# Image token products of a two-layer cross-attention on four column tiles, in two parts, with their weights loaded earlier

## The chip, the core and the metric

The kernel runs on one core of a Trainium2 chip. A core has five engines that work side by side and wait for one another by semaphores: TensorE (PE, with its weight loads listed as PEld), VectorE (DVE), ScalarE (ACT), GpSimd (POOL) and SyncE (SP, which here issues nearly all DMAs). The metric is the device time of one execution in microseconds, as a median of runs. TensorE's clock is granted at one of two levels, 2.4 GHz (1.00 in the rows) or 1.2 GHz (0.50).

## The reference

Two cross-attention layers over 8 batches of 256 tokens with 320 channels, 20 heads of 16; the context has 256 tokens with 512 channels. Layer 0 attends to the first 77 and to the other context tokens separately and adds the two. Layer 1 attends to the first 252 tokens, and to the last four (the image tokens) in a way of its own:

```python
k_ip = heads(ip_ehs @ W_k_ip)
v_ip = heads(ip_ehs @ W_v_ip)
attn_scores = jnp.einsum('bhsd,bhnd->bhsn', q, k_ip) * attn_scale
qsem = jnp.einsum('bhst,bte->bhse', probs_t, text_ehs)
qsem = _l2norm(qsem)
ip_n = _l2norm(ip_ehs)
sem = jnp.einsum('bhse,bne->bhsn', qsem, ip_n)
...
fused = attn_scores + SEM_SCALE * sem
probs_ip = jax.nn.softmax(fused, axis=-1)
...
ip_out = jnp.einsum('bhsn,bhnd->bhsd', probs_ip, v_ip)
```

The image tokens of all batches are 8 x 4 = 32 rows of 512 channels. Three small results are made of them once: their keys and values by two 512x320 weights, and their norms. The change is about these.

## The kernel before, in words

The work is cut into 16 units, eight batches of layer 0 and eight of layer 1. Each unit has ten slots j = 0 to 9; slot (u, j) handles the scores and weights of two heads of unit u, and beside them the maxima of the heads of unit u+1 and the projections of unit u+2. `plan(u, j)` (L80) writes out by hand what stands in a slot, and every engine walks through the same plan, each taking its own part of an item: PE multiplies, ACT takes exponentials (`P`) and copies results out of PSUM, DVE takes maxima and subtracts for the low parts, POOL does other differences, and SP stores queries and keys to DRAM and loads them back by heads. Nothing is reordered at run time. PE's results go to seven PSUM banks that are taken in turn; `take` waits until the earlier user of a bank has been read.

The image tokens are one item, `ip`, in slot (1, 3), behind everything else of that slot. Its function on PE is `image_tokens` (L612). For each of the two weights it makes three groups of output rows (128, 128, 64), each a sum of four matmuls with 128 rows of contraction and 32 moving columns (L620). Then come four matmuls that sum the squares `csq` over the partitions by a matrix of ones (L627), and four matmuls that give the values a second time with the tokens on the partitions (L632). All these are float32, and each such matmul appears in the trace as two instructions. ACT copies the results to `kip`, `vhi` and `vip`, DVE makes `vlo` and clips the norms (`nrm`), and POOL takes their power -0.5 (`invip`, L1329). Keys and norms are first used in layer 1.

The weights `wki1` and `wvi1` lie in the tile `Y` (128x3072), which layer 0 otherwise leaves free after the start. SP loads them (2 x 640 KB, L1357) at slot (0, 8), behind the rows of the shift (`QP<-mlo`, L746) and ahead of the key rows of unit 2 (`KP<-k0d`, L730), which the first maximum of slot (1, 0) needs (L458). Other names of the steps: L379 are the projections, L481 the scores, L513 and L517 the weighted values of a pair of slots, in which four heads stand on four column tiles of the array (`tile_position=(0, 32 * j)`), L536, L549, L553 and L469 transposes, L579 the output products of the unit before.

Of the kernel before, what the change touches and what calls it, by code (L numbers as in the profile page):

```python
# [9 lines left out]
ALU = mybir.AluOpType  # L10
# [7 lines left out]
NIP = 4  # L18
KC = 3
# [20 lines left out]
MAXF = (3, 3, 3, 3, 2, 2, 2, 2, 0, 0)  # L40
SHIFT = 7


# [36 lines left out]
def plan(u, j):  # L80
# [90 lines left out]
def build(nc, xT, cT, cipT, fs, Wq0, Wk0, Wv0, Wki0, Wvi0, Wo0, bo0,  # L171
          Wq1, Wk1, Wv1, Wki1, Wvi1, Wo1, bo1, ident_d, ind_d, hm_d, outT):
    with ExitStack() as ctx:
# [62 lines left out]
        kip = sb("kip", [128, KC, B * NIP])  # L236
        vhi, vlo = (cs[:, 96 * i:96 * i + 96].bitcast(F32R).rearrange("p (k n) -> p k n", n=B * NIP) for i in range(2))
        hmask = cs[:, 192:192 + KC * H].rearrange("p (k h) -> p k h", h=H)
        VB_all = sb("VB", [128, NIP * C])
        VB = VB_all[:, :].rearrange("p (n c) -> p n c", c=C)  # L240
        invip = sb("invip", [128, B * NIP])
        nrm = sb("nrm", [128, B * NIP])
        bdh, bdl = (VB_all[:, 240 * i:240 * i + 240].bitcast(F32R).rearrange("p (k h n) -> p k h n", k=KC, h=H) for i in range(2))
# [4 lines left out]
        rn = sb("rn", [128, 2, H])  # L248
        t1 = sb("t1", [128, 2, H, NIP])
        ex = sb("ex", [128, 2, H, NIP])  # L250
# [73 lines left out]
        def tensor_program(_):  # L324
# [5 lines left out]
            def freed(what):  # L330
                kind, a = what[0], what[1]
                if kind == "mx":
                    pe.wait_ge(dv_mx, a + 1)
                elif kind == "bg":
                    pe.wait_ge(ac_bg, job_no(a, what[2]))
                    if what[2] in LOWS[lay(a)]:
                        pe.wait_ge(dv_bg, low_no(a, what[2]))
                    if what[2] in ("G0", "G1"):
                        pe.wait_ge(dv_vg, 2 * (a - B) + 1 + (what[2] == "G1"))
                elif kind == "sc":  # L340
                    pe.wait_ge(ac_exp, 2 * a + what[2] + 1)
                elif kind == "gp":
                    pe.wait_ge(dv_y, 2 * (a - B * NP) + what[2] + 1)
                elif kind == "idle":
                    pass
                elif kind == "nt":
                    pe.wait_ge(dv_nb, a + 1)
                elif kind == "sr":
                    pe.wait_ge(ac_sr, a + 1)
                    pe.wait_ge(dv_sr, a + 1)  # L350
                elif kind == "ot":
                    pe.wait_ge(ac_ot, 2 * a + what[2] + 1)
                    pe.wait_ge(dv_ot, 2 * a + what[2] + 1)
                elif kind == "wt":
                    pe.wait_ge(ac_wt, closing_no(a))
                elif kind == "op":
                    pe.wait_ge(dv_op, 2 * a + what[2] + 1)
                elif kind == "mb":
                    pe.wait_ge(ac_mb, closing_no(a))
                elif kind == "ip":  # L360
                    pe.wait_ge(*((ac_ip, 1), (dv_ip, 1), (dv_ip, 2), (ac_ip, 3))[a])

# [248 lines left out]

            def image_tokens():  # L612
                for i, w in enumerate((wki1, wvi1)):
                    bank = take("ip", i)
                    pe.wait_ge(l_w["ip1"], 32)
                    pe.wait_ge(l_w["const"], 16 * 6)
                    for m in range(KC):
                        M = CHUNK[m]
                        for k in range(EC):
                            made = mm(bank[0:M, 32 * m:32 * m + 32], w[:, k, m * 128:m * 128 + M], cip[:, k, :],  # L620
                                      start=(k == 0), stop=(k == EC - 1))
                    made.then_inc(pe_ip, 1)
                    give(bank)
                bank = take("ip", 2)
                pe.wait_ge(dv_set, 3)
                for k in range(EC):
                    made = mm(bank[:, 0:32], ones[:, :], csq[:, k, :], start=(k == 0), stop=(k == EC - 1))  # L627
                made.then_inc(pe_ip, 1)
                give(bank)
                bank = take("ip", 3)  # L630
                for k in range(EC):
                    made = mm(bank[0:B * NIP, 0:C], cip[:, k, :], wvi1[:, k, :], start=(k == 0), stop=(k == EC - 1))  # L632
                made.then_inc(pe_ip, 1)
                give(bank)

# [10 lines left out]
            for u in range(-1, U):  # L646
                ahead = prepare(u + 2) if u + 2 < U else iter(())
                for j in range(NP):
                    for what, *a in plan(u, j):
# [7 lines left out]
                        elif what == "quad":  # L657
                            quad(*a)
                        elif what == "weigh":
                            weigh(*a)  # L660
                        elif what == "scores":
                            scores(*a)
                        elif what == "back":
                            values_back(*a)
                        elif what == "ot":
                            attention_back(*a)
                        elif what == "wt":
                            image_weights_back(*a)
                        elif what == "mb":
                            image_values(*a)  # L670
                        elif what == "op":
                            output(*a)
                        elif what == "ip":
                            image_tokens()
                for _ in ahead:
# [72 lines left out]
        def scalar_program(_):  # L748
# [25 lines left out]
            def projection(u, job):  # L774
# [15 lines left out]
                elif job[0] == "K":  # L790
# [5 lines left out]
                    else:  # L796
                        ac.wait_ge(ac_ip, 1)
                        copy(khi[0:M, cs, TXT1:S], kip[0:M, cs, NIP * b:NIP * b + NIP])
# [64 lines left out]

            def image_tokens():
                ac.wait_ge(pe_ip, 1)
                bank = bank_of["ip", 0]
                copy(kip[:, 0:2, :], bank[:, 0:64].rearrange("p (c n) -> p c n", n=32))
                copy(kip[0:64, 2, :], bank[0:64, 64:96]).then_inc(ac_ip, 1)
                ac.wait_ge(pe_ip, 4)
                bank = bank_of["ip", 1]  # L870
                copy(vhi[:, 0:2, :], bank[:, 0:64].rearrange("p (c n) -> p c n", n=32))
                copy(vhi[0:64, 2, :], bank[0:64, 64:96]).then_inc(ac_ip, 1)
                copy(vip, bank_of["ip", 3][0:B * NIP, 0:C]).then_inc(ac_ip, 1)

# [29 lines left out]
            for u in range(-1, U):  # L904
                for j in range(NP):
                    for what, *a in plan(u, j):
# [24 lines left out]
                        elif what == "ip":  # L931
                            image_tokens()
                    if u == 0 and j == 3:
# [19 lines left out]
        def vector_program(_):  # L953
# [198 lines left out]

            def image_tokens():
                dv.wait_ge(l_w["const"], 16 * 6)
                tt(csq[:, :, :], cip[:, :, :], cip[:, :, :], MUL).then_inc(dv_set, 1)
                dv.wait_ge(ac_ip, 2)
                bank = bank_of["ip", 1]
                low(vlo[:, 0:2, :], bank[:, 0:64].rearrange("p (c n) -> p c n", n=32), vhi[:, 0:2, :])
                low(vlo[0:64, 2, :], bank[0:64, 64:96], vhi[0:64, 2, :]).then_inc(dv_ip, 1)
                dv.wait_ge(pe_ip, 3)  # L1160
                nc.vector.tensor_scalar(nrm[:, :], bank_of["ip", 2][:, 0:32], 1e-24, None, ALU.max).then_inc(dv_ip, 1)

            def image_values(u):
                b = u % B
                dv.wait_ge(dv_ip, 1)
                dv.wait_ge(l_hm, 16)
# [38 lines left out]
            for u in range(-1, U):  # L1205
                for j in range(NP):
                    for what, *a in plan(u, j):
                        if what == "max":
# [27 lines left out]
                        elif what == "ip":  # L1236
                            image_tokens()
                    if u == B - 3 and j == NP - 1:
# [8 lines left out]
        def gpsimd_program(_):  # L1247
# [70 lines left out]
            for u in range(-1, U):  # L1318
                for j in range(NP):
                    for what, *a in plan(u, j):  # L1320
# [4 lines left out]
                        elif what == "mix":  # L1325
                            image_step(*a)
                        elif what == "ip":
                            po.wait_ge(dv_ip, 2)
                            tt(invip[:, :], nrm[:, :], mhalf[:, 0:B * NIP], POW).then_inc(po_ip, 1)  # L1329
# [18 lines left out]
        def sync_program(_):  # L1348
# [96 lines left out]
            for u in range(-1, U):  # L1445
                for j in range(NP):
                    for what, *a in plan(u, j):
# [17 lines left out]
                    if u == 2 and j == 3:  # L1465
                        sp.wait_ge(pe_ip, 4)
                        load_twice(sq1, Wq1, l_w["q1"])
# [5 lines left out]
                    if u == 3 and j == 0:  # L1473
                        sp.wait_ge(ac_ip, 3)
                        dma(vipd.rearrange("b (n c) -> (b n) c", c=C), vip).then_inc(l_vip, 16)
                        sp.wait_ge(pe_ip, 4)
                        dma(hmask, hm_d).then_inc(l_hm, 16)
# [93 lines left out]
```

## Time and profile before

| what | value |
|---|---|
| median of 3 runs | 816.89 us (816.88 to 821.27) |
| the profiled execution | 819.18 us, span 817.4 us |
| mean granted TensorE clock | 0.981 |
| PE busy | 782.5 us, 96% |
| DVE busy | 560.0 us, 69% |
| ACT busy | 425.0 us, 52% |
| POOL busy | 402.6 us, 49% |
| chain that ended last, PE's share | 76% |

The span is from the first to the last instruction of the profiled execution; its time has 1.8 us around that. Times in rows are counted from the start of the span. PE is busy in nearly every slice of the page, and the other engines in parts. The page of the whole run hides the place of the change, which is 12 us out of 817, so the rows below are of stretches around 80 to 130 us, and of the same place two units later.

### The profile page before, as it was taken

To read this page: it belongs to the slowest core of one execution; us is meant where nothing else is said; L and a number is where in the kernel's file an instruction comes from. 1 tells how busy PE (TensorE), PEld (TensorE's weight loads), DVE (VectorE), ACT (ScalarE), POOL (GpSimd) and SP (SyncE) were. 2 spreads that over 40 slices of the span, in tenths; PEclk is the share of its full clock that TensorE was granted. 3 is DMA by queue.
4 is the path that set the end of the run, shared out by engine and by line. 5 is a ranking of instruction groups with operands and counts; after the bars stand their busy time and mean duration, and the time that the engine had idled before them with its cause. 6 is when DMAs were issued, how large, how long until landed. Compare 5 with 4: busy or idle time off the path is not lost.

```text
span 817.4 us, 17243 instructions
## 1 busy us (share of the span) xinstructions
PE 782.5 (96%) x6392; PEld 635.2 (78%) x6392; DVE 560.0 (69%) x1531; ACT 425.0 (52%) x911; POOL 402.6 (49%) x297
## 2 busy tenths in 40 slices
PE   5989899999999999999999999999999999988896
PEld 5877787888888878787877778787887888766574
DVE  5357345757575857677858778788697797687744
ACT  5234523655546474646465465565555655555551
POOL 6421202201102040403658976887779768779763
PEclk9999989999999999999999999999999999999998
DMA  8975631847546564546443345245062342500010
GB/s 266 219 210 151 178 111 54 227 135 190 128 146 162 179 153 132 158 118 159 114 112 121 94 108 167 64 113 156 35 184 86 86 116 66 139 1 16 21 34 16
DMA packets 103027, 100.67 MB, mean 123 GB/s; under 512 B 10264, under 2 KB 102176, under 8 KB 102944
## 3 DMA queue, kind: packets, MB, share of 16 engines
q1 hardware_dynamic: 101408, 98.26, 43.5%
q10 hardware_dynamic: 1536, 1.31, 0.5%
q8 instruction: 51, 0.84, 0.4%
q14 instruction: 32, 0.26, 0.1%
HBM read 61.65 MB, written 36.74 MB: 120 GB/s over the span
## 4 chain that ended last, share of the span: by engine, by line
PE 76%; DVE 7%; issue 4%; DMA 4%; POOL 4%; ACT 3%; SPq 2%; POOLq 0%; DVEq 0%; ACTq 0%
PE pB L379 22%; PE pB L495 13%; PE pB L458 8%; PE pB L481 7%; PE pB L579 5%; PE pPV L522 4%; PE pPV L517 4%; PE pPV L527 4%; PE pB L536 3%; POOL Y L1278 3%; PE pPV L513 2%; DMA KP<-k0d 2%; DVE m_sb L1041 2%; DVE m_sb L1043 1%; ACT P L842 1%
## 5 line engine op out<-in xcount | busy, mean ns | idle before, releaser
L1278 POOL TENSOR_TENSOR Y<-P,wv 128x512 f32<-128x512 f32 x120 | 156.5, 1321 | 106.8 <-ACT P L842 106.6
L1058 DVE TENSOR_TENSOR Y<-pB,Y 128x512 f32<-128x512 f32 x160 | 108.8, 686 | 70.5 <-PE pB L495 60.6
L458 PE MATMUL pB<-KP,QP 96*128 96x256 f32 x640 | 129.8, 288 | 4.4 <-DMA KP<-k0d 3.2
L458 PEld LDWEIGHTS pB<-KP,QP 96*128 96x128 f32 x640 | 106.6, 191 | 18.4 <-issue 7.4
L1255 POOL TENSOR_TENSOR klo<-xin,khi 128x256 fp32r<-128x256 f32 x18 | 13.3, 758 | 216.8 <-ACT khi L753 216.8
L1043 DVE TENSOR_REDUCE m_sb<-pB 128x2 f32<-128x504 f32 x160 | 108.0, 675 | 11.2 <-PE pB L458 9.5
L481 PE MATMUL pB<-QP,KP 100*128 100x512 f32 x320 | 109.2, 421 | 2.4 <-DMA QP<-mlo 2.0
L842 ACT ACTIVATE P<-pB 128x512 f32<-128x512 f32 x160 | 86.5, 596 | 43.7 <-PE pB L481 33.8
L842 ACT ACTIVATE P<-pB,ln 128x512 f32<-128x512 f32 x160 | 101.3, 692 | 0.0
L832 ACT ACTIVATE wv<-pB 128x512 fp32r<-128x512 f32 x120 | 66.8, 591 | 56.6 <-PE pB L481 55.3
L753 ACT ACTIVATE Vs<-pPV 128x512 f32<-128x512 f32 (+1 forms) x80 | 39.4, 493 | 101.5 <-PE pPV L517 68.2
L1041 DVE TENSOR_REDUCE m_sb<-pB 128x2 f32<-128x358 f32 x160 | 83.2, 520 | 0.0
L1040 DVE TENSOR_REDUCE m_sb<-pB 128x2 f32<-128x154 f32 x160 | 49.7, 311 | 45.9 <-PE pB L458 45.3
L495 PE MATMUL pB<-wv,wk 128*128 128x512 f32 x250 | 76.8, 410 | 0.5
L379 PE MATMUL pB<-chi,wki 128*128 128x180 f32 (+3 forms) x384 | 72.0, 274 | 0.0
L379 PE MATMUL pB<-khi,wq 128*128 128x256 f32 (+1 forms) x288 | 56.8, 293 | 8.6 <-DVE wq L960 8.6
L1301 POOL TENSOR_TENSOR rn<-n,mhalf 128x8 f32<-128x8 f32 (+2 forms) x17 | 57.1, 3358 | 15.8 <-DVE n L1089 15.8
L379 PE MATMUL pB<-wvi,chi 128*128 128x320 f32 x256 | 62.0, 312 | 0.2 <-POOL wvi L1268 0.2
L379 PEld LDWEIGHTS pB<-chi,wki 128*128 128x128 f32 (+1 forms) x384 | 56.3, 172 | 6.0 <-issue 4.1
L495 PEld LDWEIGHTS pB<-wv,wk 128*128 128x128 f32 x250 | 44.2, 190 | 18.9 <-issue 10.3
L481 PEld LDWEIGHTS pB<-QP,KP 100*128 100x128 f32 x320 | 50.2, 191 | 6.6 <-DMA QP<-mlo 2.5
L379 PEld LDWEIGHTS pB<-khi,wq 128*128 128x128 f32 (+1 forms) x288 | 44.0, 182 | 12.3 <-DVE wq L960 8.6
(175 smaller groups left out, 1718.2 us busy)
## 6 DMA issues: line engine op xcount, KB each, us to landing
QP<-q0d SPq DMA_DIRECT2D x64, 192.0 KB, 4.1
KP<-k0d SPq DMA_DIRECT2D x64, 192.0 KB, 4.4
c_sb<-in_cT SPq DMA_DIRECT2D x16, 512.0 KB, 5.2
q0d<-qhi SPq DMA_DIRECT2D x32, 256.0 KB, 2.5
k0d<-khi SPq DMA_DIRECT2D x30, 256.0 KB, 2.5
q0d<-qlo SPq DMA_DIRECT2D x16, 256.0 KB, 2.8
k0d<-klo SPq DMA_DIRECT2D x15, 256.0 KB, 2.8
VB<-vipd SPq DMA_DIRECT2D x6, 640.0 KB, 3.9
```

The costliest lines, as they stand in the source:

```text
L379: made = mm(out, l, r, start=(n == 0), stop=(n == len(pairs) - 1))
L458: made = mm(bank[:, sc * S:sc * S + S], QP[i][0:KROWS, j, a, sc * 128:sc * 128 + 128], KP[i][0:KROWS, j, :], start=True, stop=True)
L481: mm(bank[:, :], KP[i][0:QROWS, j, ch * 128:ch * 128 + 128], QP[i][0:QROWS, j, :, :].rearrange("p a s -> p (a s)"), start=True, stop=True) ...
L495: made = mm(bank[:, :], G[i][:, col:col + 128], ph[src], start=(n == 0), stop=(n == len(jobs) - 1))
L832: act(PH[q % HR][ch], bank_of["sc", q, ch][:, :], ACT.Exp, scale=0.25).then_inc(ac_ph, 1)
L842: act(P[:, q % PR, ch, :], bank_of["sc", q, ch][:, :], ACT.Exp, scale=0.25, **twice).then_inc(ac_exp, 1)
L1040: nc.vector.tensor_reduce(m_sb[:, :, h], v[:, :, 0:TXT0], AX, ALU.max)
L1041: nc.vector.tensor_reduce(m_sb[:, :, H + h], v[:, :, TXT0:S], AX, ALU.max).then_inc(dv_mx, 1)
L1043: nc.vector.tensor_reduce(m_sb[:, :, h], v[:, :, 0:TXT1], AX, ALU.max)
L1058: tt(Y[:, p, dst, :], bank_of["gp", q, dst][:, :], Y[:, p, dst, :], MUL).then_inc(dv_y, 1)
L1278: tt(Y[:, p, ch, :], P[:, p, ch, :], PH[q % HR][ch].bitcast(F32), SUB).then_inc(po_y, 1)
L1301: tt(rn[:, :, hs], n2[:, :, hs], mhalf[:, 0:2 * n].rearrange("p (c h) -> p c h", c=2), POW).then_inc(po_rn, 1)
```

## The change

The item `ip` becomes two items: part 0 in slot (1, 0) and part 1 in slot (1, 2).

Part 0 makes the products the other way round: the 32 tokens are the weights and the 320 columns of `wki1` or `wvi1` move. The four parts of the contraction are no longer summed in PSUM. Each stands on a column tile of its own, so a bank holds four partial sums, one under another on 4 x 32 partitions. ACT copies the two banks into `Y`, over the first of the four parts of each weight. The norms are one matmul with 128 moving columns, and DVE sums the four parts of its result.

Part 1 sums the partial sums and transposes them in one step: a matmul with the partial sums as weights and `stack`, four 32x32 identities one under another, as moving columns. DVE makes `stack` from the identity at the start of slot (0, 9), in the tile `t1`, together with the squares. One more matmul, with `stack` as weights, gives the values with the tokens on the partitions.

SP issues the loads of the two weights at slot (0, 5) instead of (0, 8).

```diff
+IP_AT = ((1, 0), (1, 2))
...
-    if (u, j) == (1, 3):
-        out += [("ip",)]
+    if (u, j) in IP_AT:
+        out += [("ip", IP_AT.index((u, j)))]
...
+        stack = t1_all[:, 0:B * NIP]
+        parts = [Y_flat[:, EC * C * i:EC * C * i + C] for i in range(2)]
...
-            def image_tokens():
-                for i, w in enumerate((wki1, wvi1)):
-                    bank = take("ip", i)
-                    pe.wait_ge(l_w["ip1"], 32)
-                    pe.wait_ge(l_w["const"], 16 * 6)
-                    for m in range(KC):
-                        M = CHUNK[m]
+            def image_tokens(part):
+                if part == 0:
+
+                    for i, w in enumerate((wki1, wvi1)):
+                        bank = take("ip", i)
+                        pe.wait_ge(l_w["ip1"], 32)
+                        pe.wait_ge(l_w["const"], 16 * 6)
                         for k in range(EC):
-                            made = mm(bank[0:M, 32 * m:32 * m + 32], w[:, k, m * 128:m * 128 + M], cip[:, k, :],
-                                      start=(k == 0), stop=(k == EC - 1))
-                    made.then_inc(pe_ip, 1)
+                            made = mm(bank[32 * k:32 * k + 32, 0:C], cip[:, k, :], w[:, k, :], start=True, stop=True,
+                                      tile_position=(0, 32 * k))
+                        made.then_inc(pe_ip, 1)
+                        give(bank)
+                    bank = take("ip", 2)
+                    pe.wait_ge(dv_set, 3)
+                    mm(bank[:, 0:128], ones[:, :], cs[:, 128:256], start=True, stop=True).then_inc(pe_ip, 1)
                     give(bank)
...
+                else:
+
+                    pe.wait_ge(dv_set, 4)
+                    for i in range(2):
+                        bank = take("ip", 3 + i)
+                        pe.wait_ge(ac_ip, i + 1)
+                        for m in range(KC):
+                            M = CHUNK[m]
+                            made = mm(bank[0:M, 32 * m:32 * m + 32], parts[i][:, m * 128:m * 128 + M], stack, start=True, stop=True)
+                        made.then_inc(pe_ip, 1)
+                        give(bank)
+                    bank = take("ip", 5)
+                    mm(bank[0:B * NIP, 0:C], stack, parts[1], start=True, stop=True).then_inc(pe_ip, 1)
+                    give(bank)
...
+            def image_tokens(part):
+                if part == 0:
+                    for i in range(2):
+                        ac.wait_ge(pe_ip, i + 1)
+                        copy(parts[i], bank_of["ip", i][:, 0:C]).then_inc(ac_ip, 1)
...
+            def image_sums():
                 dv.wait_ge(l_w["const"], 16 * 6)
+                dv.wait_ge(l_w["ident"], 16)
                 tt(csq[:, :, :], cip[:, :, :], cip[:, :, :], MUL).then_inc(dv_set, 1)
...
+                nc.vector.tensor_reduce(stack, ident[:, :].rearrange("p (k n) -> p n k", n=B * NIP), AX, ADD).then_inc(dv_set, 1)
+
+            def image_tokens(part):
+                if part == 0:
+                    dv.wait_ge(pe_ip, 3)
+                    then(nc.vector.tensor_reduce(nrm[:, :], bank_of["ip", 2][:, 0:128].rearrange("p (k n) -> p n k", n=B * NIP), AX, ADD))
+                    settled()
+                    nc.vector.tensor_scalar(nrm[:, :], nrm[:, :], 1e-24, None, ALU.max).then_inc(dv_ip, 1)
...
-                    if u == 0 and j == 8:
+                    if u == 0 and j == 5:
                         sp.wait_ge(lo_w["o0"], 1)
                         sp.wait_ge(lo_w["k0"], 1)
                         sp.wait_ge(ac_set, 2)
                         load512(wki1, Wki1, l_w["ip1"])
                         load512(wvi1, Wvi1, l_w["ip1"])
```

Semaphore numbers elsewhere follow (the copies of ACT count to 5 instead of 3), and the orders below show where the items stand. The first place is on PE at the end of slot (1, 3). `cs` holds `cip` and the squares, `Y` the weights. Before:

```order
L458 MATMUL pB<-KP,QP 128x256 x2
L620 MATMUL pB<-cs,Y 128x32 x8
L620 MATMUL pB<-cs,Y 64x32 x4
L620 MATMUL pB<-cs,Y 128x32 x8
L620 MATMUL pB<-cs,Y 64x32 x4
L627 MATMUL pB<-cs,ones 128x32 x4
L632 MATMUL pB<-Y,cs 32x320 x4
L481 MATMUL pB<-QP,KP 128x512 x2
```

These 32 matmuls are gone from there, and the scores of slot (1, 4) follow the last maximum of (1, 3). Now on PE at the end of slot (1, 0), with the line numbers of the changed kernel (L463 are the maxima, L541 the transposes, L486 the scores):

```order
L463 MATMUL pB<-KP,QP 128x256 x4
L541 MATMUL pB<-ident,Vs 128x128 x4
L625 MATMUL pB<-Y,cs 32x320 x8
L631 MATMUL pB<-cs,ones 128x128
L486 MATMUL pB<-QP,KP 128x512 x2
```

and at the end of slot (1, 2), where `t` is the tile `t1` with the stacked identities and `Y` the partial sums:

```order
L541 MATMUL pB<-ident,Vs 128x128 x4
L558 MATMUL pB<-ident,O 64x128 x2
L641 MATMUL pB<-t,Y 128x32 x2
L641 MATMUL pB<-t,Y 64x32
L641 MATMUL pB<-t,Y 128x32 x2
L641 MATMUL pB<-t,Y 64x32
L645 MATMUL pB<-Y,t 32x320
L486 MATMUL pB<-QP,KP 128x512 x2
```

PE has 9 matmuls in the one place and 7 in the other, instead of 32. The last place is SP's queue in unit 0. Before, behind the key stores of unit 2:

```order
L702 DMA k1d<-khi 64x256 x2
L702 DMA k1d<-klo 64x256
L746 DMA QP<-mlo 1x20x256 x2
L1357 DMA Y<-in_Wki 128x4x320
L1357 DMA Y<-in_Wvi 128x4x320
L730 DMA KP<-k0d 48x4x256 x2
```

and now:

```order
L714 DMA k1d<-khi 64x256 x2
L714 DMA k1d<-klo 64x256
L1385 DMA Y<-in_Wki 128x4x320
L1385 DMA Y<-in_Wvi 128x4x320
L758 DMA QP<-mlo 1x20x256 x2
L742 DMA KP<-k0d 48x4x256 x2
```

The two weight loads have moved past the shift rows, and nothing stands between those and the keys any more.

## Rows read from the trace of the kernel before

**Rows 1.** The page, part 1: busy time, share of the span, instructions.

```profile
PE 782.5 (96%) x6392; PEld 635.2 (78%) x6392; DVE 560.0 (69%) x1531; ACT 425.0 (52%) x911; POOL 402.6 (49%) x297
```

**Rows 2.** Windows: length, busy us of PE, PEld, DVE, ACT, POOL, clock, DMA, GB/s.

```profile
166.67:204.08 37.41, 37.41 (x345) 31.80 (x345) 24.75 (x75) 19.93 (x45) 4.26 (x6) 1.00 0.57 155
...
85.71:129.22 43.51, 41.40 (x323) 32.88 (x323) 17.57 (x54) 17.67 (x42) 8.45 (x7) 0.88 0.48 128
176.09:204.08 27.99, 27.99 (x259) 23.56 (x259) 17.05 (x50) 16.65 (x37) 4.26 (x6) 1.00 0.63 167
```

**Rows 3.** The chain that ended last, slots (1, 1) to (1, 4): start, us, what.

```profile
103.83 0.47 PE pB L481 x2
...
104.74 0.57 PE pPV L513 x8
105.31 0.87 PE pPV L517 x16
...
111.75 6.13 PE pB L620 x48
117.88 1.85 PE pB L627 x8
119.73 4.41 PE pB L632 x8
124.14 1.08 PE pB L481 x2
```

**Rows 4.** Windows around two falls of the clock.

```profile
80.60:84.00 3.40, 3.40 (x28) 1.94 (x21) 1.20 (x4) 1.04 (x3) 0.00 (x0) 0.50 0.56 167
111.59:114.62 3.03, 3.03 (x32) 2.95 (x30) 1.56 (x6) 0.30 (x2) 0.00 (x0) 1.00 0.19 48
114.62:125.00 10.38, 10.38 (x38) 6.93 (x38) 0.41 (x3) 0.73 (x3) 0.00 (x1) 0.51 0.00 0
```

**Rows 5.** Waits of PE from 92 to 129: us, times, longest.

```profile
PE pB L458 <- DMA KP<-k0d: 2.1, 1, 2.1
```

**Rows 6.** Timeline of PE: start, us, instruction, idle before and its releaser.

```profile
91.62 0.71 PE L481 MATMUL pB<-QP,KP 100*128 100x512 f32 x2
...
98.36 0.47 PE L458 MATMUL pB<-KP,QP 96*128 96x256 f32 x2 [2.11 <-DMA KP<-k0d]
...
186.72 0.40 PE L458 MATMUL pB<-KP,QP 96*128 96x256 f32 x2
```

**Rows 7.** Single lines: durations in ns (min/median/max), first and last start.

```profile
L620 PE MATMUL pB<-cs,Y x24: 195/276/276, 111.6 to 113.8; 128*128 128x32 f32 x16, 128*64 128x32 f32 x8
...
L517 PEld LDWEIGHTS pPV<-P,VY x48: 107/110/113, 104.9 to 135.8; 128*32 128x32 f32 x48
```

**Rows 8.** Timeline of SP's queue, and one row of POOL.

```profile
82.07 0.60 SPq L702 DMA_DIRECT2D k1d<-klo  x1
87.34 1.67 SPq L746 DMA_DIRECT2D QP<-mlo  x2
...
90.12 1.38 SPq L730 DMA_DIRECT2D KP<-k0d  x2
...
179.62 1.26 SPq L730 DMA_DIRECT2D KP<-k0d  x2
...
72.79 0.86 POOL L1266 TENSOR_TENSOR wo<-Y,wo 64x320 fp32r<-64x320 f32 x1
```

**Rows 9.** Window between the key stores and the old place of the loads.

```profile
84.20:89.10 4.90, 4.90 (x43) 4.05 (x45) 2.12 (x7) 1.66 (x4) 0.00 (x0) 1.00 0.03 8
```

**Rows 10.** DMA issues, us to landing: 89 to 100, then the page.

```profile
KP<-k0d SPq DMA_DIRECT2D x4, 192.0 KB, 7.3
Y<-in_Wvi SPq DMA_DIRECT2D x1, 640.0 KB, 5.7
...
KP<-k0d SPq DMA_DIRECT2D x64, 192.0 KB, 4.4
```

**Rows 11.** Groups of instructions on ACT, 94 to 130: busy us, mean ns.

```profile
L753 ACT ACTIVATE kt<-pB 32x320 f32<-32x320 f32 x1 | 0.4, 427 | 0.0
```

More of the change, by code:

```diff
@@ L673, in tensor_program @@
                         elif what == "ip":
-                            image_tokens()
+                            image_tokens(*a)
                 for _ in ahead:
@@ L862, in image_weights @@
                 act(ex[:, :, :, :], t1[:, :, :, :], ACT.Exp, scale=0.25).then_inc(ac_ex, 1)
[L864 to L873, printed above, removed]
+            def image_tokens(part):
[3 more added lines that the diff above has]
+                        copy(parts[i], bank_of["ip", i][:, 0:C]).then_inc(ac_ip, 1)
+                else:
+                    ac.wait_ge(pe_ip, 4)
+                    bank = bank_of["ip", 3]
+                    copy(kip[:, 0:2, :], bank[:, 0:64].rearrange("p (c n) -> p c n", n=32))
+                    copy(kip[0:64, 2, :], bank[0:64, 64:96]).then_inc(ac_ip, 1)
+                    ac.wait_ge(pe_ip, 5)
+                    bank = bank_of["ip", 4]
+                    copy(vhi[:, 0:2, :], bank[:, 0:64].rearrange("p (c n) -> p c n", n=32))
+                    copy(vhi[0:64, 2, :], bank[0:64, 64:96]).then_inc(ac_ip, 1)
+                    ac.wait_ge(pe_ip, 6)
+                    copy(vip, bank_of["ip", 5][0:B * NIP, 0:C]).then_inc(ac_ip, 1)
             def image_weights_back(u):
@@ L1151, in last_output @@
                                                    ADD, ADD).then_inc(dv_op, 1)
-            def image_tokens():
+            def image_sums():
                 dv.wait_ge(l_w["const"], 16 * 6)
+                dv.wait_ge(l_w["ident"], 16)
                 tt(csq[:, :, :], cip[:, :, :], cip[:, :, :], MUL).then_inc(dv_set, 1)
[L1156 to L1161, printed above, removed]
+                nc.vector.tensor_reduce(stack, ident[:, :].rearrange("p (k n) -> p n k", n=B * NIP), AX, ADD).then_inc(dv_set, 1)
[5 more added lines that the diff above has]
+                    nc.vector.tensor_scalar(nrm[:, :], nrm[:, :], 1e-24, None, ALU.max).then_inc(dv_ip, 1)
+                else:
+                    dv.wait_ge(ac_ip, 4)
+                    bank = bank_of["ip", 4]
+                    low(vlo[:, 0:2, :], bank[:, 0:64].rearrange("p (c n) -> p c n", n=32), vhi[:, 0:2, :])
+                    low(vlo[0:64, 2, :], bank[0:64, 64:96], vhi[0:64, 2, :]).then_inc(dv_ip, 1)
             def image_values(u):
                 b = u % B
-                dv.wait_ge(dv_ip, 1)
+                dv.wait_ge(dv_ip, 2)
                 dv.wait_ge(l_hm, 16)
@@ L1206, in vector_program @@
                 for j in range(NP):
+                    if (u, j) == (0, 9):
+                        image_sums()
                     for what, *a in plan(u, j):
@@ L1326, in gpsimd_program @@
                             image_step(*a)
-                        elif what == "ip":
-                            po.wait_ge(dv_ip, 2)
+                        elif what == "ip" and a[0] == 0:
+                            po.wait_ge(dv_ip, 1)
                             tt(invip[:, :], nrm[:, :], mhalf[:, 0:B * NIP], POW).then_inc(po_ip, 1)
```

29 lines of the change are left out of this document (10 added, 19 removed).

## The prediction

> **What bounds the kernel now.** I read the page first: TensorE (PE) is busy 96% of the span [rows 1]. To see whether that is a real bound in the stage around the change, I asked the view by windows for whole units of 37.4 us. Unit 2 to 3 is 37.41 us long and PE is busy for all of it at full clock [rows 2]; its neighbours up to 278.9 us read the same, within 0.05 us. So what PE does not have to do here comes off the end, unless a wait takes its place.
>
> Then the chain of waits, where the image token block stands: 111.75 to 124.14 us, three groups of matmuls with nothing between them, 12.39 us in all [rows 3]. The windows tell why it is so long for so little: PE began it at full clock, and from 114.62 to 125.00 the granted clock was 0.51, the lower level of 1.2 GHz, after 3 us in which PE did nothing but 32-column products [rows 4]. The pair of scores behind it took 1.08 us where a pair at full clock takes 0.47 [rows 3], so 0.61 us more belong to it. Between 92 and 129 us PE waited once: 2.1 us for the keys of unit 2 [rows 5].
>
> A check from above: from the transposes of the shift in unit 0 (85.71) to the output products in unit 1 (129.22) are 43.51 us; the same work two units on takes 27.99 us [rows 2]. The excess is 15.5 us, and 12.39 + 0.61 + 2.11 = 15.1 us of it are named.
>
> **The change: what PE gives up and gets.** Given up: 12.39 + 0.61 = 13.0 us.
>
> Part 0, products: 8 matmuls of 320 columns, in two rounds of four column tiles. A float32 matmul shows as two instructions, so they are 16. The nearest row is L517: 16 instructions of 256 columns on four column tiles, two rounds, take 0.87 us at full clock [rows 3]. Times 320/256: 1.09 us. The block before had the same products as L632, 8 instructions of 320 columns one after the other, 4.41 us at half clock [rows 3], so about 2.2 at full clock; done one after the other, two weights would take 4.4 us. That is the upper bound.
>
> Here a page bears on it. The L517 row holds its weight loads: they last 110 ns each [rows 7], 16 of them are 1.76 us, and the 16 matmuls still take 0.87, so they lie beside one another. The Trainium skill (TensorE: Matmul & The Clock Gate, "What overlaps and what doesn't") says that a load overlaps running matmuls only where the row group differs, which column tiles don't offer; by that part 0 would be some 1.8 us dearer, 2.9 instead of 1.1, an estimate. The trace disagrees with this, and I go by the row.
>
> Part 0, norms: one matmul with 128 columns, two instructions. In L517 a tile streams 256 columns in 0.87/4 = 0.22 us per instruction, so 128 columns take 0.11, and two instructions 0.22; I take 0.25 us.
>
> Part 1: half of L620. Its first 24 instructions (two thirds of 128 weights, one third of 64) ran at full clock from 111.75 until about 113.95, where the copy of kip starts, so 92 ns each [rows 3, 7]; 12 of them are 1.10 us. One matmul of 320 columns follows, two instructions at half of 551 ns (L632 at half clock, 4.41/8): 0.55 us.
>
> Changing between whole array and tiles: L513 is one round of four, 0.57 us where 0.44 is streamed [rows 3], 0.13 us more; twice that, 0.25 us, for entering and leaving.
>
> Sum for PE: 1.09 + 0.25 + 1.10 + 0.55 + 0.25 = 3.24 us. Bounds: 2.7 with nothing for changes and norms, 6.6 if the tiles do not run beside one another. PE work falls by 13.0 - 3.24 = 9.8 us.
>
> **The change: the loads.** SP issued Wki and Wvi (1.28 MB) between the shift rows and the keys of unit 2. Now they go out behind the key stores, at about 82.7 us, where SP issues nothing until 87.34 [rows 8]. The waits ahead of them hold nothing: the newest is for the low part of wo, which POOL finished at 73.7 [rows 8]. The DMA engines were 3% busy from 84.2 to 89.1 [rows 9], and the later load of the pair landed 5.7 us after issue [rows 10], so now by 89. Two things stand behind them on the queue. The shift rows, issued at 87.34 and read by the scores at 91.62 [rows 6, 8]: they lose at most what is left of the pair, 0 to 1 us of some 2. The keys: their issue moves from 90.12 to about 89.1, and 1.28 MB less lie ahead of them. They landed 7.3 us after issue where the median is 4.4 [rows 10]. Issued at 89.1 and 89.7 they land at about 94.3, and PE asks at 96.25. The same distance two units on, issue at 179.62, first use at 186.72, 7.1 us, is without a wait [rows 6, 8]. So all of the 2.1 us goes [rows 5, 6].
>
> **What is hidden.** ACT gets two copies of 128x320; one of as many columns took 0.43 us [rows 11]. They stand behind the weights of slot (1,0), where ACT had nothing to do until the next scores, and part 0 delays those by more than the copies last. If that cover were gone they would cost 0.9 us. DVE gets two reduces of 128x128, one of them (identity) with the square of cip where DVE stood idle, as PE waited for keys. The other (norms) stands before the maxima of slot (1,1), where DVE is nearly full. No row has that reduce; the bounds are nothing and 0.7 us, what a maximum over 504 columns takes on the page. PE has 1.3 us of part 0 meanwhile, so I take nothing. POOL's power of the norms comes some 25 us sooner, and nothing in this layer reads it.
>
> What is late next? After the block PE had 11 us in which DVE, ACT and DMA caught up. The units without a block show that they need no such pause [rows 2]. I take 0 for it.
>
> **Sum.** 9.8 + 2.1 = 11.9 us. The profiled execution took 819.18 us with a span of 817.4, so 807.3 and 805.5. The runs shown have a median of 816.89, 2.3 below the profiled one; I predict in their terms: 816.89 - 11.9 = 805.0 us, 1.5% less.
>
> **The rivals.** (a) Forecast, 0.62.
> (b) The clock falls again. Part 1 has the same products before which it fell, and six transposes just ahead. For: it also fell at 80.6 us, where PE was short of work for moments only. Against: it fell 3 us into the old block [rows 4], and part 1 is 1.7 us with a 320-column matmul in it. That fall held for 3.4 us, PE busy at half speed [rows 4]: price 1.7 us, 806.7. Chance 0.15.
> (c) The wait for keys or rows stays, since SP's issue time and the row transfers bound it: 2.1 us, 807.1. Against it are the 7.1 us above. 0.08.
> (d) The tiles run one after another: 4.4 instead of 1.1 us, 808.3. Against it is L517. 0.05.
> (e) Something that does not follow PE catches up, such as the transfers for units 3 and 4, which had 10 us of quiet DMA beside the block [rows 4]. Half of the gain lost would give 811. Against it: two units on the same transfers move with the DMA engines 63% busy, and PE never waits [rows 2]. 0.07.
> (f) Slower. The one way is the clock: every us at 1.2 GHz costs half a us, so it takes more than 24 us of it to eat 11.9 us, and 34 us would give 822. That would need part 0's tiles to count for nothing too and the low clock to last over slots (1,0) to (1,9). L517 in every second slot with the clock at 1.00 [rows 2] speaks against it. 0.03.
>
> **The numbers.** About 1% is what a measurement of this kernel can tell from no change; that bound is 808.7 us. (a) to (c) lie below it, (d) on it, (e) within 1%, (f) beyond on the other side: faster 0.86, same 0.11, slower 0.03. The range takes in (a) with 1.5 us less for cheap switches, the excess of 0.4 us that no row named and the unsteadiness of a median, 803.2, and reaches over (b), (c) and (d) to 808.8. The likeliest case alone spans 803.5 to 806.
>
> **What would show it.** Right: L625 with 16 instructions in about 1.1 us; L641 and L645 in 1.7 us; a granted clock of 1.00 from 92 to 130 us; no wait of PE for KP near 96; scores and output products of unit 1 (L579 before) at about 117.3 instead of 129.2; units of 37.4 us behind it [rows 2]. Wrong: a window at 0.5 behind part 1 (b), a wait on QP or KP near 92 or 96 (c), L625 above 2 us (d), a new PE wait after 120 us (e).

## The result, and the profile after

The changed kernel takes 810.37 us as a median of 10 runs (808.14 to 816.1); the kernel before, timed beside it, 818.73 us (10 runs). The ratio is 0.990, with a 95% interval of 0.988 to 0.992, so 6.4 to 9.6 us are gained. The forecast was 11.9 us, 805.0 us, with a range that ended at 808.8: the direction was right, the size was not. Of the 5.4 us between 805.0 and 810.37, 1.8 are that the kernel before was at 818.73 here and not at 816.89; 3.5 are gain that did not come. Here and below, executions more than 1.5% above the fastest of their kernel are left out of ratios and intervals. The profiled execution took 811.3 us with a span of 809.5, and the same kernel, repeated later as e4, took 810.1 us, so the figure is steady.

The page of after, its first rows, to be laid beside [rows 1]:

```profile
span 809.5 us, 17185 instructions
...
PE 771.5 (95%) x6360; PEld 626.8 (77%) x6360; DVE 562.1 (69%) x1533; ACT 426.0 (53%) x913; POOL 402.2 (50%) x297
```

TensorE has 11 us less to do, DVE and ACT 2.1 and 1.0 us more, and the span is 7.9 us shorter. Now the chain of waits through unit 0's end and unit 1 (start, us, what), where [rows 3] stood:

```profile
87.78 0.85 SPq L758
88.67 5.52 DMA QP<-mlo
94.24 0.74 PE pB L486 x2
...
98.90 0.24 PE pB L463 x2
...
100.79 1.21 PE pB L625 x16
102.00 0.42 PE pB L631 x2
102.42 0.46 PE pB L486 x2
...
110.98 1.39 PE pB L641 x12
112.37 0.66 PE pB L645 x2
113.03 0.66 PE pB L486 x2
...
120.21 1.91 PE pB L584 x16
```

The three groups of 12.39 us are gone. In their place stand 1.21 + 0.42 + 1.39 + 0.66 = 3.68 us, and the scores behind part 1 took 0.66 us where a pair at full clock takes 0.47 [rows 3]. With these 0.19 us it is 3.87 us against the 3.24 of the forecast. The output products of unit 1 start at 120.21 instead of 129.22 [rows 2]. But a transfer now stands in the chain that was not there: 5.52 us of the shift rows. The waits of PE from 84 to 130 us (us, times, longest), where [rows 5] had the keys:

```profile
PE pB L486 <- DMA QP<-mlo: 1.9, 1, 1.9
```

The wait for keys before the maximum L463 at 98.90 is gone, as forecast. A wait of nearly the same length stands 5 us ahead of it, for the rows of the shift. SP's queue shows why, against [rows 8]:

```profile
84.12 0.60 SPq L714 DMA_DIRECT2D k1d<-klo  x1
84.81 0.53 SPq L1385 DMA_DIRECT2D Y<-in_Wki  x1
85.39 0.54 SPq L1385 DMA_DIRECT2D Y<-in_Wvi  x1
87.78 1.68 SPq L758 DMA_DIRECT2D QP<-mlo  x2
89.50 1.26 SPq L742 DMA_DIRECT2D KP<-k0d  x2
```

The rows were issued 2.4 us behind the second load. That load took 7.1 us to land, and the keys behind took 5.6, from the DMA issues between 82 and 100 us (as in [rows 10]):

```profile
KP<-k0d SPq DMA_DIRECT2D x4, 192.0 KB, 5.6
Y<-in_Wki SPq DMA_DIRECT2D x1, 640.0 KB, 4.3
Y<-in_Wvi SPq DMA_DIRECT2D x1, 640.0 KB, 7.1
```

and the traffic in the 8 us from 84.72, in 40 slices of 0.2 us:

```profile
GB/s 189 133 5 133 179 16 77 166 51 38 58 160 288 378 403 397 384 378 403 371 397 397 397 397 397 403 381 291 240 103 15 67 87 236 179 67 51 61 72 82
```

The loads' 1.28 MB flow at some 390 GB/s from about 87.1 to 90.5 us. So they came to full rate about 2.5 us after the first issue, and the rows, issued at 87.78 and 88.67, met them in full flow. Wvi landed at 92.5, the rows at 94.2. The clock was not part of it in this execution; the windows from 84 us on (length, busy us of PE, PEld, DVE, ACT, POOL, clock, DMA, GB/s):

```profile
84.00:95.00 11.00, 9.06 (x73) 7.38 (x74) 4.39 (x14) 6.58 (x15) 1.40 (x2) 1.00 0.89 209
95.00:108.00 13.00, 13.00 (x129) 9.87 (x129) 8.45 (x25) 7.55 (x18) 7.75 (x5) 1.00 0.68 168
108.00:119.00 11.00, 11.00 (x95) 9.25 (x96) 6.09 (x19) 5.40 (x15) 0.51 (x1) 1.00 0.45 122
```

PE is busy 9.06 of the first 11 us; the 1.94 us missing are the wait. Everything behind is full, at full clock.

### The profile page after: what moved, and what is told of

Same layout as the page of the kernel before. It is cut to its first block, busy times and chain, and to the rows that moved or that the text cites. A ratio compares the mean times of both kernels' runs of the same rounds, so it can differ in the third digit from the quotient of the medians.

```text
span 809.5 us, 17185 instructions
## 1 busy us (share of the span) xinstructions
PE 771.5 (95%) x6360; PEld 626.8 (77%) x6360; DVE 562.1 (69%) x1533; ACT 426.0 (53%) x913; POOL 402.2 (50%) x297
## 4 chain that ended last, share of the span: by engine, by line
PE 75%; DVE 9%; issue 4%; DMA 4%; POOL 3%; ACT 3%; SPq 1%; POOLq 0%; DVEq 0%; ACTq 0%
PE pB L384 22%; PE pB L500 12%; PE pB L463 8%; PE pB L486 8%; PE pB L584 5%; PE pPV L527 4%; PE pPV L522 4%; PE pPV L532 4%; PE pB L541 3%; PE pPV L518 3%; POOL Y L1306 2%; DVE m_sb L1061 2%; DVE m_sb L1059 2%; DMA QP<-mlo 1%; DMA Y<-in_Wk 1%
## 5 line engine op out<-in xcount | busy, mean ns | idle before, releaser
L463 PE MATMUL pB<-KP,QP 96*128 96x256 f32 x640 | 130.2, 288 | 2.7 <-DMA KP<-k0d 1.6
L463 PEld LDWEIGHTS pB<-KP,QP 96*128 96x128 f32 x640 | 107.1, 192 | 16.5 <-issue 5.8
L486 PE MATMUL pB<-QP,KP 100*128 100x512 f32 x320 | 108.3, 418 | 5.1 <-DMA QP<-mlo 4.4
L854 ACT ACTIVATE P<-pB 128x512 f32<-128x512 f32 x160 | 86.5, 597 | 42.0 <-PE pB L486 32.1
L486 PEld LDWEIGHTS pB<-QP,KP 100*128 100x128 f32 x320 | 50.0, 190 | 9.2 <-DMA QP<-mlo 5.2
L384 PEld LDWEIGHTS pB<-khi,wq 128*128 128x128 f32 (+1 forms) x288 | 44.5, 183 | 12.7 <-DVE wq L978 9.0
```

The lines of the kernel that those rows point to most:

```text
L384: made = mm(out, l, r, start=(n == 0), stop=(n == len(pairs) - 1))
L463: made = mm(bank[:, sc * S:sc * S + S], QP[i][0:KROWS, j, a, sc * 128:sc * 128 + 128], KP[i][0:KROWS, j, :], start=True, stop=True)
L486: mm(bank[:, :], KP[i][0:QROWS, j, ch * 128:ch * 128 + 128], QP[i][0:QROWS, j, :, :].rearrange("p a s -> p (a s)"), start=True, stop=True) ...
L854: act(P[:, q % PR, ch, :], bank_of["sc", q, ch][:, :], ACT.Exp, scale=0.25, **twice).then_inc(ac_exp, 1)
```

## The experiments

To compare executions I use one stretch, from the first transpose of `Vs` behind 82 us (L536 before, 85.19 us; L541 after, 85.64) to the first output product of unit 1 (128.98 before, 119.96 after), both by the timeline of PE. It is 43.8 us in the profile before and 34.3 in the one after. The table has all runs; the last columns are of each run's one profiled execution: this stretch, PE's wait for a DMA in it, and us of the stretch from 90 us on in which the clock was low, as near as its windows show. Each ratio is against the kernel before, timed beside that run; the median of those was 819.09 us beside e1 to e4, 821.0 beside e5 to e8 and 819.5 beside e9 to e11, so ratios can be compared across these groups and medians only within one.

| run | ratio, 95% interval | stretch | wait, for | low clock |
|---|---|---|---|---|
| before | 1 | 43.8 | 2.1, keys | 10.2 |
| e5, before again | 1.000 (0.998 to 1.003) | 40.6 | 2.0, keys | 3.4 |
| e6, before again | one run, 823.55 us | 45.3 | 2.2, keys | 3.4 and 10.2 |
| after | 0.990 (0.988 to 0.992) | 34.3 | 1.9, rows | none |
| e4, after again | 0.989 (0.986 to 0.992) | 35.8 | 1.8, rows | 3.4 |
| e1, loads only | 0.998 (0.996 to 1.000) | 40.3 | 1.7, rows | 3.4 |
| e2, products only | 0.991 (0.988 to 0.993) | 36.2 | 2.2, keys | 3.4 |
| e3, after, loads at (0, 4) | 0.984 (0.980 to 0.987) | 32.1 | none | none |
| e10, the same again | 0.985 (0.982 to 0.988) | 32.1 | none | none |
| e11, one load at (0, 4), one at (0, 5) | 0.986 (0.983 to 0.989) | 32.2 | none | none |
| e9, before, loads at (0, 4) | 0.995 (0.993 to 0.998) | 38.4 | none | 3.4 |
| e7, old products in three slots | 0.995 (0.993 to 0.997) | 34.6, and 2.3 behind it | 2.0, keys | 3.4 |
| e8, part 0 on one tile | 0.997 (0.995 to 0.999) | 42.3 | 1.8, rows | 3.4 and 6.8 |

**The two halves apart (e1, e2).** e1 is the kernel before with this alone:

```diff
-                    if u == 0 and j == 8:
+                    if u == 0 and j == 5:
                         sp.wait_ge(lo_w["o0"], 1)
```

> The kernel before, with only the two weight loads moved from slot (0, 8) to (0, 5). Theory 1 (the wait only changes its name): the 1.28 MB now lie ahead of the shift rows on SP's queue, PE waits about 2 us for QP<-mlo at the scores of slot (0, 9) and no longer for KP<-k0d at the first maximum of slot (1, 0); the sum of the two waits is within 0.5 us of 2.1 us, and the time equals that of the kernel before within its noise. Rival 2 (the wait for the rows in the changed kernel came from its new matmuls or from chance): no wait for rows here, PE waits for nothing between 84 and 110 us, and the kernel gains about 2.1 us.

Measured: 817.95 us (12 runs), ratio 0.998, at most 3.4 us gained and perhaps 0.3. The waits of PE in e1, 84 to 130 us:

```profile
PE pB L481 <- DMA QP<-mlo: 1.7, 1, 1.7
```

So the loads at (0, 5), without the new products, already swap the keys' wait of 2.0 to 2.2 us for one of 1.7 for the rows. That is nearly all they do.

e2 is the changed kernel with the opposite edit, loads back at (0, 8).

> The changed kernel with the two loads put back to slot (0, 8). Theory 1: PE waits 2.1 us for KP<-k0d in slot (1, 0) as before, none for the rows, the new matmuls take 3.7 us as in the changed kernel, and the time equals that of the changed kernel within 0.5 us plus noise: the whole gain comes from the products. Rival 2: the early loads carry part of the gain, and this kernel is 2 us slower than the changed one. Part 0 may in addition wait for the weights, which landed 5.7 us after issue at 89.6; it needs them at about 100, so no such wait is expected.

Measured: 812.25 us (6 runs), ratio 0.991. The products alone bring the gain, and the keys' wait is back (2.2 us). In the profiled execution the clock was low right behind that wait, from 98.7 for 3.4 us, into part 0, whose L625 took 1.62 instead of 1.21 us.

**Where the loads must stand (e3, e10, e11, e9).** e3 is the changed kernel with one number changed:

```diff
-                    if u == 0 and j == 5:
+                    if u == 0 and j == 4:
                         sp.wait_ge(lo_w["o0"], 1)
```

> The changed kernel with the two loads one slot sooner still, at (0, 4), so that they stand ahead of the key stores of unit 2 and not behind them. SP issues them when POOL has finished the low part of wo, at about 74 us, and they land by 80, while the DMA engines are at 14% from 75 to 80. Theory 1: neither the rows nor the keys are late, PE waits for nothing from 84 to 110 us, and the output products of unit 1 stand about 1.9 us sooner after the scores of slot (0, 7) than in the changed kernel; the end moves by 1 to 1.9 us. Rival 3 (the row transfers are slow by themselves): the wait for QP<-mlo stays at 1.5 us or more.

Measured: 806.87 us (5 runs), ratio 0.984. In the repeat:

> The changed kernel with the loads at (0,4), the same as in the run e3, repeated beside the others. Theory: the whole stretch from 84 to 130 us without a wait and without a low clock, ratio 0.984 to 0.987, which is the 2.5 to 3 us that the wait behind the loads costs with its scores and clock, below the 0.989 of the changed kernel. Rival: e3 was a lucky series of the start-up and the end; then 0.987 to 0.991.

Measured: 806.97 us (5 runs), ratio 0.985. The two medians are 3.1 to 3.5 us below the changed kernel's two, and every run of e3 (808.42 at most) is below every run of e4 (809.38 at least), timed beside it. So the first series was no luck. The gain over the kernel before is 12.2 and 12.5 us by the medians, with intervals of 10.6 to 16.4 and 10.2 to 14.4: with the loads at (0, 4), the 11.9 us of the forecast are there. SP's queue in e10:

```profile
74.05 0.37 SPq L1385 DMA_DIRECT2D Y<-in_Wki  x1
74.46 0.51 SPq L1385 DMA_DIRECT2D Y<-in_Wvi  x1
78.82 1.71 SPq L712 DMA_DIRECT2D k0d<-khi  x2
...
82.44 0.60 SPq L714 DMA_DIRECT2D k1d<-klo  x1
87.70 1.68 SPq L758 DMA_DIRECT2D QP<-mlo  x2
```

and its windows:

```profile
84.00:95.00 11.00, 11.00 (x98) 8.85 (x101) 4.47 (x14) 7.34 (x17) 1.43 (x2) 0.99 0.42 96
95.00:108.00 13.00, 13.00 (x127) 10.58 (x116) 9.12 (x27) 7.86 (x18) 8.27 (x5) 1.00 0.62 170
```

The second load took 5.3 us and landed at about 79.8, 8 us before the rows are issued, and PE is busy for all 11 us where after had 9.06. The key rows landed in 4.1 us. This is a version faster than both kernels.

e11 asks whether the bytes ahead of the rows make the wait, or something else about rows behind key stores. One weight is loaded at (0, 4), the other at (0, 5).

```diff
-                    if u == 0 and j == 5:
+                    if u == 0 and j == 4:
                         sp.wait_ge(lo_w["o0"], 1)
                         sp.wait_ge(lo_w["k0"], 1)
                         sp.wait_ge(ac_set, 2)
                         load512(wki1, Wki1, l_w["ip1"])
+                    if u == 0 and j == 5:
                         load512(wvi1, Wvi1, l_w["ip1"])
```

> The changed kernel with one weight loaded at (0,4) and the other at (0,5): 0.64 MB instead of 1.28 MB stand ahead of the shift rows. If the wait for the rows is made by the bytes ahead of them, it goes by about 0.64 MB at 390 GB/s, 1.65 us: a wait of 0.2 us at most instead of 1.8 to 1.9, and a ratio near that of both loads at (0,4). Rival: it is the issue time or the row transfers themselves that are slow when keys are stored shortly before; then 1.8 us are left whatever the bytes.

Measured: 809.2 us (4 runs), ratio 0.986. SP's queue in e11:

```profile
82.50 0.60 SPq L714 DMA_DIRECT2D k1d<-klo  x1
83.14 0.59 SPq L1385 DMA_DIRECT2D Y<-in_Wvi  x1
86.18 1.68 SPq L758 DMA_DIRECT2D QP<-mlo  x2
```

The rows still follow one load on the same queue, and the distance from the key store to the rows is the same 3.7 us as in after. Yet no wait is left. In the timeline of PE the scores of that slot start 4.4 us behind the rows' issue, with no idle time ahead of them:

```profile
90.55 0.73 PE L486 MATMUL pB<-QP,KP 100*128 100x512 f32 x2
```

The bytes ahead make the wait. The kernels with both loads behind the rows agree: e2, e5, e6 and e7 have the same 3.7 us between key store and rows, and no wait for the rows. By time alone e11 cannot be told from the changed kernel, since the intervals overlap (0.983 to 0.989 and 0.988 to 0.992); the profile decides here.

e9 is the kernel before with the loads at (0, 4), so the wait is taken away with the old products in place.

> The kernel before with the loads at (0,4), ahead of the key stores; the products stay as they were in (1,3). It gives the loads' share alone when nothing is behind them. My theory (the loads at (0,5) only rename the wait, and at (0,4) it goes): no wait of PE between 84 and 110 us, and a ratio of about 0.995 to 0.996 (2.1 us of wait, 0.3 us of slowed scores, and the low clock that follows a wait in some executions), against 0.998 of the loads at (0,5). The block itself still takes 9.7 to 12.7 us by the clock. Rival: the wait was never worth its 2 us, since the pause helps what comes later; then 0.998 to 1.000 again, with no wait near 96 but new ones behind it.

Measured: 815.3 us (median of 9 runs), ratio 0.995, and no wait of PE from 84 to 110 us. So the wait with what hangs on it is worth 2.0 to 6.1 us; loads at (0, 5), in e1, got 0.3 to 3.4. These two intervals overlap, and it is the profiles that tell the two places apart. The rival, that a pause there helps what comes later, falls: the interval ends at 0.998, and no new wait stands in the stretch.

**How steady the old block was (e4, e5, e6).** These are the changed kernel and, twice, the kernel before, unedited.

> The changed kernel, unaltered, as a control on the same chip. It tells which differences between the two profiles are of the kernel and which of the execution: theory 1 expects the wait for the rows of 1.9 us again within 0.3 us and a span from the output products of unit 1 to the end that varies by up to 1.5 us with where the clock falls in the last 100 us; if the 1.0 us that was lost between unit 1 and the end is of the kernel (rival 4: something downstream takes back a part of the gain), it shows again here in full.

Measured: 810.1 us (6 runs), ratio 0.989, wait 1.8 us again, and here the clock was low from 94.0 for 3.4 us behind it, so the stretch is 1.5 us longer than in the first profile.

> The kernel before, unaltered, for a second profile of it. Theory A (the cost of the old block is unsteady, since it depends on how long the clock stays down): the block of L620, L627 and L632 with the scores behind it takes another time than the 13.5 us of the first profile, down to about 10 us, where less of it lies at the lower clock. Rival B (the block costs the same each time): 13.5 us within 0.3, with the clock at 0.5 for 10 us again.

> The same again, one look, for a third profile: theory A expects the block's time to lie anywhere from 8 to 13.5 us, rival B 13.5 us.

Measured: ratio 1.000 in e5, and 823.55 us in the one run of e6. The chain in e5, and then in e6, of the block that [rows 3] has with 12.39 us:

```profile
110.91 4.77 PE pB L620 x48
115.69 1.10 PE pB L627 x8
116.79 3.81 PE pB L632 x8
```

```profile
112.68 6.43 PE pB L620 x48
119.11 1.85 PE pB L627 x8
120.95 4.41 PE pB L632 x8
```

The same 64 instructions took 9.68 us in one execution and 12.69 in the other. The windows say what differs: in e5 the clock was low for 3.4 us, from 116.5; in e6 it was low over all but the first 2.7 us. The second row here, of e6, has nearly all of that:

```profile
112.68:115.70 3.02, 3.02 (x31) 2.94 (x29) 1.40 (x5) 0.30 (x2) 0.00 (x0) 0.95 0.14 46
115.70:125.36 9.66, 9.66 (x37) 6.31 (x36) 0.00 (x0) 0.00 (x0) 0.00 (x0) 0.50 0.00 0
```

Of five executions with the old block (before, e1, e5, e6, e9) three took 9.7 us, two 12.4 and 12.7. The block that I took as a constant is a draw.

**What the clock costs in it (e7).** The old products, unchanged, in three slots: keys by `wki1` in (1, 3), norms and the values with tokens on partitions in (1, 4), values by `wvi1` in (1, 5).

```diff
+IP_AT = ((1, 3), (1, 4), (1, 5))
...
-    if (u, j) == (1, 3):
-        out += [("ip",)]
+    if (u, j) in IP_AT:
+        out += [("ip", IP_AT.index((u, j)))]
...
```

> The kernel before with its old matmuls, all of them and in their old form, but in three portions at the ends of slots (1, 3), (1, 4) and (1, 5): the keys' 12 products, then norms and the values by tokens, then the values' 12 products; the loads stay at (0, 8). Theory 1 (of the 13.0 us that were removed the clock is a large part): at full clock the portions take 2.2, 0.9 + 2.2 and 2.2 us, 7.5 in all, so the kernel gains up to 5.5 us on the first profile, with PE's clock at 1.00 through them. Rival 2 (it is the number of matmuls that costs): the portions together take 12 us or more and nothing is gained.

Measured: 815.59 us (12 runs), ratio 0.995 (0.993 to 0.997). The chain in e7:

```profile
111.33 2.29 PE pB L622 x24
...
120.20 0.81 PE pB L630 x8
121.02 2.27 PE pB L635 x8
...
126.63 2.29 PE pB L622 x24
```

The same work takes 7.66 us at full clock. So of the 12.39 us that I took off, some 4.7 were the low clock. Merely spacing the products out brings about half of what the new form brings with the loads in the same place (0.995 against 0.991 in e2, the middles of their intervals). The new form saves 7.66 - 3.68 = 4.0 us of work.

**What the tiles bring (e8).** The changed kernel, but the four products of part 0 are summed on one tile of 32 columns, one behind another, and part 1 reads 32 partitions.

```diff
-                            made = mm(bank[32 * k:32 * k + 32, 0:C], cip[:, k, :], w[:, k, :], start=True, stop=True,
-                                      tile_position=(0, 32 * k))
+                            made = mm(bank[0:32, 0:C], cip[:, k, :], w[:, k, :], start=(k == 0), stop=(k == EC - 1))
...
```

> The changed kernel without column tiles: part 0 sums its four matmuls for each weight in PSUM on one 32-column tile, part 1 uses 32 rows of contraction instead of 128. Theory 1 (the four tiles run beside one another): part 0's products take 4.4 us instead of 1.2, so the kernel is 3.2 us slower than the changed one; part 1 stays at 2.05 us. Rival 2 (what was gained is the swap of weights and moving columns, and the tiles bring nothing): 1.2 to 1.5 us here too.

Measured: 817.64 us (12 runs), ratio 0.997 (0.995 to 0.999). In its chain:

```profile
99.44 4.42 PE pB L625 x16
103.86 0.42 PE pB L630 x2
...
112.86 1.57 PE pB L640 x12
114.42 0.65 PE pB L644 x2
```

and a window right behind part 1:

```profile
116.90:123.70 6.80, 6.80 (x43) 4.66 (x43) 2.27 (x6) 0.91 (x2) 0.00 (x0) 0.52 0.00 0
```

The 16 instructions take 4.42 us instead of 1.21, at full clock both times: the upper bound of the forecast (4.4) to the digit. That is 3.2 us. By the ratios e8 lies 5.7 to 6.9 us behind the changed kernel (0.997 against 0.990 and 0.989). In the profiles its stretch is 8.0 us longer than in after; beside the 3.2 us the clock was low there for 3.4 us from 92.7, behind the wait for rows, and for 6.8 us from 116.7, behind part 1, which costs half of these 10.2 us. So a fall behind part 1, as in rival (b), does occur in a denser form of this work; that the tiles are what keeps it away is not separated here.

## Why the prediction was wrong, and where it was right

**The step that failed** is the one on the loads: "they lose at most what is left of the pair, 0 to 1 us of some 2", and from it "so all of the 2.1 us goes". The rows cost 1.94 us of PE's time in place of nothing. (The scores behind the wait, 0.74 us, are no part of it: the same pair took 0.71 before [rows 6] and 0.73 in e11, both without a wait. The "0.3 us of slowed scores" in the expectation of e9 is this misreading.) Three things under the step were wrong:

1. "the later load of the pair landed 5.7 us after issue [rows 10], so now by 89". In the new place it took 7.1 us in after, 6.8 in e1, 6.7 in e4 and 6.6 in e8. I read a landing time in one place of the queue and used it in another; the keys' stores had only just been issued there.
2. The distance. In the profile before, the rows were issued 5.3 us behind the last key store (82.07 to 87.34, [rows 8]). In after, e1 to e8 and e11 it is 3.7 us. The one profile I had was stretched exactly there by a low clock from 80.60 to 84.00, which stood in [rows 4] before me; I used it as a price for a rival and did not see that it also made the room for the loads. (e9 and e10, with a low clock between 80 and 87, show 5.2 and 5.3.) The idle DMA of [rows 9] was the same stretched place. Had the rows been issued 1.6 us later here too, some 0.3 of the 1.94 us would have been left, inside the 0 to 1 us of the forecast; that is an estimate, and no run shows it.
3. What counts for a transfer behind the loads is the bytes ahead of it, not its own size: 40 KB of rows waited for 1.28 MB. e11 shows this, since with 0.64 MB ahead the wait is gone.

Rival (c), the wait for keys or rows stays, had a chance of 0.08 and was the case. "Against it are the 7.1 us" spoke of the keys only, which did behave as said; nothing spoke against the rows. Its price of 2.1 us was right.

**What a wait brings with it** was missing altogether. Of nine profiled executions with a wait of 1.7 to 2.2 us between 90 and 99 us, five (e2, e4, e6, e7, e8) had the clock low right behind it for 3.4 us, which costs 1.7 us of work; of the four without a wait (e3, e9, e10, e11) none had, from 90 to 108 us. This fits that loads at (0, 4) gain 3.1 to 3.5 us over the changed kernel, where the wait is 1.9. But if wait and clock had nothing to do with each other, all five of thirteen would still fall among the nine about one time in ten, so it is a hint and not shown.

**New products: 3.24 forecast, 3.87 measured**, inside the bounds of 2.7 to 6.6. Part 0 was 1.21 for 1.09. The norms were 0.42 for 0.25. Why is open: their weight load waited 0.5 us for a maximum of DVE in after, but in e2 and e8, without that wait, they took 0.42 us too. Part 1 was 1.39 for 1.10 and 0.66 for 0.55, and 0.19 are in the scores behind. The 0.25 us for switching were in these.

**Given up: 13.0 us** was right for that execution and not for all: 9.7 + 0.66 in e1, e5 and e9. Over the five executions with the old block its mean is 10.8 us and not 12.39, so as a term for the median this one was some 1.6 us too large; it is the second mis-sized step, and one profile could not show it. The mean of the stretch over three executions of before is 43.2 us, over two of the changed kernel 35.0: 8.2 us, which is what the medians show. Measured like the 43.8 of the profile before, the forecast's stretch was 43.8 - 11.9 = 31.9; without the wait (e3, e10) it is 32.1. Against that one profile the sum was right to some 0.2 us but for the one step, partly by luck, since the new products were 0.6 us dearer than in the sum.

**The balance** in the two profiles: 11.9 - 1.9 (rows) - 0.6 (products) = 9.4 us, and the stretch is 43.8 - 34.3 = 9.5 us shorter. The span is 7.9 us shorter. Of the other 1.6 us, 0.5 lie ahead of the stretch and 1.1 behind it. Those behind are not taken back by the change: from the first output product of unit 1 to the end of the span it is 688.4, 690.9 and 691.9 us in three executions of the kernel before (before, e5, e6) and 689.5 and 689.0 in two of the changed one. What varies is, for one, a wait of PE for DVE's `w` near the end, 1.5 us in after, 1.6 in e5 and e11, none in before and e10. In the medians (8.0 us with 6.4 to 9.6) the clock behind the wait in some executions, 1.5 us in e4, is in its place; that attribution is by two profiles and is not settled.

**Right:** the keys' wait gone, and the tiles beside one another. L625's 16 weight loads last up to 110 ns each, 1.76 us in sum, and its 16 matmuls took 1.21 us with them. Nor is this a matter of tiles alone: in all of after, matmuls are 771.5 us and weight loads 626.8 us of a span of 809.5. The Trainium skill (TensorE: Matmul & The Clock Gate, "What overlaps and what doesn't") lets a load lie beside matmuls only where the row group differs, which made an estimate of 2.9 us; the trace does not agree with it here. Rival (b) did not occur in after, e3, e4, e10 or e11, nor (d). The hidden work stayed hidden. ACT's two copies took 438 ns each. DVE's reduction, for which I had bounds of 0 and 0.7 us:

```profile
L1180 DVE TENSOR_REDUCE nrm<-pB x1: 281/281/281, 102.5 to 102.5; 128x32 f32<-128x128 f32 x1
```

and POOL's power took 5.4 us and nobody waited for it. The 0 for what is late next holds too: in e3, without a wait, PE is busy for all of 84 to 280 us, so rival (e) falls.

## What to carry to other kernels

Before a bulk load is moved ahead on a queue, ask of every small transfer that then stands behind it when the load's last byte is through, not when its own bytes would be: 40 KB behind 1.28 MB cost as much as the wait that was to go, and one slot further ahead (e3, e10) cost nothing. Slack read from a single profile has to be checked for a low clock in the same place, since that stretches the compute and makes room for transfers which is not there in other executions; two more profiles of the kernel before would have shown 3.7 us instead of 5.3. And where a block runs at half clock, measure it several times and once spread over slots: here spreading alone (e7) brought about half of the products' gain.

## What the runs showed of the hardware that was not expected

- A load's data did not move at once: about 2.5 us from the first issue to the first full-rate slice in after, then about 3.3 us at 390 GB/s for 1.28 MB, and 2 us more until it counted as landed.
- Eight float32 matmuls of 320 columns (16 instructions) take 1.21 us in two rounds on four column tiles, and 4.42 us one behind another in e8, 3.7 times as long, with weight loads of the same 110 ns.
- Low clock came in stretches of 3.4, 6.8 and 10.2 us, in five of nine executions right behind a wait of about 2 us, and in all five with the old block within its 64 instructions, and at different places in executions of one kernel.
